# Sums of a softmax over 32 columns instead of 64, at another place, in a two-layer attention kernel

## The reference

```python
xn = _group_norm(xf, gamma, beta)
qkv = jnp.einsum('oc,bcl->bol', w_qkv, xn) + b_qkv[None, :, None]
q, k, v = jnp.split(qkv, 3, axis=1)           # each to (b*8, 64, 1024)
weight = jnp.einsum('bct,bcs->bts', q * scale, k * scale)
weight = jax.nn.softmax(weight.astype(jnp.float32), axis=-1)
a = jnp.einsum('bts,bcs->bct', weight, v)
hid = jnp.einsum('oc,bcl->bol', w_proj, a.reshape(b, c, L)) + b_proj[None, :, None]
return (xf + hid).reshape(b, c, h, w)
```

## Time and profile before

| | us |
|---|---|
| median of 3 runs | 2539.09 |
| the profiled execution | 2540.45 |
| its span, first to last instruction | 2537.3 |
| PE busy | 2466.6 (97%) |
| DVE busy | 1728.9 (68%) |
| POOL busy | 1234.4 (49%) |
| ACT busy | 1161.3 (46%) |

### The profile page before, as it was taken

One profiled execution on the slowest core, in us unless ns is written; L12 is line 12 of the kernel. 1 busy time (PEld: TensorE's weight loads), 2 busy tenths in 40 slices (PEclk: granted clock), 3 DMA queues, 4 the chain that ended last, 5 costly groups with the idle time before them and its releaser, 6 DMA issues.

```text
span 2537.3 us, 37438 instructions
## 1 busy us (share of the span) xinstructions
PE 2466.6 (97%) x12980; PEld 1618.3 (64%) x12980; DVE 1728.9 (68%) x2226; ACT 1161.3 (46%) x1499; POOL 1234.4 (49%) x621
## 2 busy tenths in 40 slices
PE   7999999999799999999999999999999999999987
PEld 6887888878555575557556655755565565557544
DVE  6455554546568866885787588578857866885776
ACT  3332232322355535654555455355555645553553
POOL 3330000000066746774766567377656756771762
PEclk9999999999899999999999999999999999999999
DMA  5431111013221141114022220502230241202001
GB/s 191 141 108 50 50 66 66 33 50 116 88 79 50 76 183 50 83 49 176 26 100 104 104 108 17 207 26 83 92 133 26 100 169 56 84 30 104 17 17 67
DMA packets 64185, 214.15 MB, mean 84 GB/s; under 512 B 9152, under 2 KB 9152, under 8 KB 63168
## 3 DMA queue, kind: packets, MB, share of 16 engines
q1 hardware_dynamic: 49504, 159.41, 17.1%
q0 software_dynamic: 14560, 52.96, 5.7%
HBM read 141.05 MB, written 71.30 MB: 84 GB/s over the span
## 4 chain that ended last, share of the span: by engine, by line
PE 82%; issue 8%; POOL 4%; DVE 3%; ACT 2%; POOLq 0%; ACTq 0%; DVEq 0%
PE psum L1258 16%; PE psum L1445 14%; PE psum L1507 14%; PE psum L1489 11%; PE psum L1277 7%; PE psum L1456 5%; POOL a_all L566 4%; PE psum L1301 4%; PE psum L1329 3%; PE psum L1521 3%; PE psum L1375 1%; ACT a_all L783 1%; PE psum L1269 1%; PE psum L1543 1%; PE psum L1389 1%
## 5 line engine op out<-in xcount | busy, mean ns | idle before, releaser
L566 POOL TENSOR_TENSOR a_all<-a_all 128x1024 f32<-128x1024 f32 x441 | 1059.9, 2403 | 500.2 <-ACT a_all L783 462.4
L783 ACT ACTIVATE a_all<-psum 128x1024 f32<-128x1024 f32 x512 | 496.6, 1022 | 65.8 <-PE psum L1489 51.9
L1507 PE MATMUL psum<-a_all 128*64 128x512 f32 x2048 | 495.7, 605 | 0.0
L1069 DVE TENSOR_REDUCE small<-psum 128x2 f32<-128x1024 f32 x326 | 399.7, 1226 | 125.6 <-PE psum L1456 123.1
L1258 PE MATMUL psum<-r_all 128*128 128x512 f32 x1920 | 455.8, 396 | 6.9 <-DVE r_all L1148 5.8
L1489 PE MATMUL psum<-r_all 64*128 64x512 f32 x3200 | 423.6, 395 | 4.5 <-ACT a_all L783 2.3
L1258 PEld LDWEIGHTS psum<-r_all 128*128 128x128 f32 x1920 | 360.4, 190 | 103.1 <-DVE r_all L922 10.2
L1445 PE MATMUL psum<-r_all 128*128 128x512 f32 x1536 | 372.2, 399 | 5.5 <-DVE r_all L1166 5.5
L1489 PEld LDWEIGHTS psum<-r_all 64*128 64x128 f32 x3200 | 295.5, 185 | 92.1 <-ACT a_all L783 35.6
L1445 PEld LDWEIGHTS psum<-r_all 128*128 128x128 f32 x1536 | 284.4, 189 | 104.2 <-issue 42.9
L1507 PEld LDWEIGHTS psum<-a_all 128*64 128x64 f32 x2048 | 124.0, 136 | 235.2 <-issue 170.7
(11 more groups left out here) (144 smaller groups left out, 2495.5 us busy)
## 6 DMA issues: line engine op xcount, KB each, us to landing
r_all<-w_dram SPq DMA_DIRECT2D x48, 1024.0 KB, 4.9
xn_dram<-a_all POOLq DMA_DIRECT2D x56, 512.0 KB, 5.4
r_all<-xn_dram SPq DMA_DIRECT2D x7, 4096.0 KB, 15.4
a_all<-y_dram SPq DMA_DIRECT2D x9, 2048.0 KB, 8.6
a_all<-x SPq DMA_DIRECT2D x16, 1024.0 KB, 6.4
y_dram<-a_all SPq DMA_DIRECT2D x16, 1024.0 KB, 4.2
out<-a_all SPq DMA_DIRECT2D x32, 512.0 KB, 4.0
w_dram<-a_all POOLq DMA_DIRECT2D x16, 512.0 KB, 3.0
```

Of the source, the lines that this page charges most:

```text
L566: pool.tensor_tensor(p_sum[:, :, cols], probs[:, 0, :, cols] if i == 1 else p_sum[:, :, cols], probs[:, i % SLOTS, :, cols], ALU.add).then ...
L783: act.activation(probs[:, i % SLOTS, :, cols], psum[half][:, :, :], ACT.Exp, scale=SCALE).then_inc(probs_ready, 1)
L1069: dve.reduce_max(max2[:, :, tile, half], psum[3][:, :, :], AX_X).then_inc(work_free, 2)
L1507: last = pe.matmul(psum[2][h * D:(h + 1) * D, half], v_t[:, i, head], probs[:, i % SLOTS, h, half * HALF:(half + 1) * HALF], start=(i == 0 ...
```

## The change

- `sums` makes four products of 32 columns instead of 64. Product k (head k // 2, half k % 2 of the queries) writes partitions 32k to 32k + 31 of one bank. The last pair of all keeps the old form.
- Its place: in pairs 1 to 3 behind the first score tile (bank psum[2][:,0]); in the last pair of the last batch behind the third (psum[3][:,0]); for pair 3 behind the third value tile instead of the second, into psum[2][:,0].
- ACT copies 128x512 to a new tile sums4, behind the first score tile's exps. DVE inverts it in 4 pieces. SP then issues 8 DMAs per pair (`spread`), each of 32 partitions x 512 floats, from sums4 to the two 32-partition parts of recip that hold one head and half. `normalise` waits for them (recip_spread).
- The first two output tiles of a batch (but the last) are made in two parts: both take their banks first, then each gets the products over the first three blocks of hid, then each the last.
- The mask is [128, 8] float32, read with stride 0, instead of [128, 1024] bfloat16.
- Waits: the first score tile no longer waits for `sums_copied`; the second key tile of a pair does, for an older copy, and the first value product does for this one.

```diff
@@ sync: issued in the middle of pairs 1 to 3, and behind the residual's load
+            def spread(b, p):
+                pairs = b * PAIRS + p
+                sp.wait_ge(sums_inverted, (pairs + 1) * PIECES)
+                sp.wait_ge(o_normed, NORMED0 + pairs * NH)
+                for k in range(2 * NH):
+                    for r in range(2):
+                        at = k // NH * D + r * QUARTER
+                        sp.dma_start(recip[at:at + QUARTER, k % NH], sums4[k * QUARTER:(k + 1) * QUARTER]).then_inc(recip_spread, 16)
@@ scalar
-                act.wait_ge(o_normed, NORMED0 + pairs * NH)
+                act.wait_ge(recip_spread, ONE + pairs * SPREAD)
                 act.wait_ge(sums_full, ONE + pairs + 1)
-                act.activation(recip, psum[1][:, :, :], ACT.Copy).then_inc(sums_copied, 1)
+                act.activation(sums4, of, ACT.Copy).then_inc(sums_copied, 1)
...
-                        if p and i == 2:
-                            copy_sums(b, p - 1)
...
+                        if p and more and i == 0:
+                            copy_sums(b, p - 1, psum[2][:, 0])
+                        if p and not more and i == 2:
+                            copy_sums(b, p - 1, psum[3][:, 0])
@@ vector
-                            if p and (m == 1 or m and m % 2 == 0):
-                                invert_sums(b, p - 1, m // 2, 1)
+                            if p and m in (2, 4, 6, 8):
+                                invert_sums(b, p - 1, m // 2 - 1, 1)
...
-                        if 1 <= i <= 4:
-                            invert_sums(b, PAIRS - 1, 2 * (i - 1), 2)
+                        if i in (2, 3):
+                            invert_sums(b, PAIRS - 1, 2 * (i - 2), 2)
                         if i == 5:
                             for h in range(NH):
                                 normalise(b, PAIRS - 1, h)
@@ tensor
-                for half in range(NH):
-                    for h in range(2):
-                        last = pe.matmul(psum[1][h * D:(h + 1) * D, half], ones64, p_sum[:, h, half * HALF:(half + 1) * HALF],
-                                         start=True, stop=True)
+                for k in range(2 * NH):
+                    h, half = k // NH, k % NH
+                    to = psum[1][h * D:(h + 1) * D, half] if last else to_bank[k * QUARTER:(k + 1) * QUARTER]
+                    done = pe.matmul(to, ones64[:, 0:D if last else QUARTER], p_sum[:, h, half * HALF:(half + 1) * HALF],
+                                     start=True, stop=True)
...
-                    if p:
-                        sums(pairs - 1)
                     next_qk(3)
                     next_max()
                     for i in range(NT):
                         scores(pairs, par, i, more)
+                        if p and more and i == 0:
+                            pe.wait_ge(k_free[1], pairs + 2)
+                            sums(pairs - 1, psum[2][:, 0])
+                        if p and not more and i == 2:
+                            sums(pairs - 1, psum[3][:, 0])
...
+                if not last:
+                    pe.wait_ge(ws_loaded[0], (loads + 3) * 16)
+                    hid_made(PAIRS - 1, NH - 1)
+                    banks = [next_tile() for _ in range(NH)]
+                    for (o, half), to in zip(tiles, banks):
+                        proj_steps(to, o, half, range(CT - 1))
+                    for (o, half), to in zip(tiles, banks):
+                        hid_made(PAIRS, half)
+                        proj_steps(to, o, half, (CT - 1,)).then_inc(work_full, 1)
```

More of the change, by code:

```diff
@@ L23 @@
 F32R = mybir.dt.float32r
-BF16 = mybir.dt.bfloat16
 ALU = mybir.AluOpType
@@ L450, in batch1 @@
                     load_y(b + 2)
+                spread(b, 0)
                 sp.wait_ge(qk_hi_done, qk_used(b, 2))
@@ L467, in batch1 @@
                 sp.dma_start(res32, y_v[b]).then_inc(res_loaded, 16)
+                if not last:
+                    spread(b, PAIRS - 1)
                 for o in range(CT):
@@ L1128, in normalise @@
                     dve.wait_ge(o_ready, ONE + pairs + 1)
-                dve.wait_ge(sums_inverted, pairs * PIECES + (h + 1) * CT)
+                if last:
+                    dve.wait_ge(sums_inverted, pairs * PIECES + h + 1)
+                elif h == 0:
+                    dve.wait_ge(recip_spread, ONE + (pairs + 1) * SPREAD)
                 o32 = o32s[:, p % 2, cols]
@@ L1509, in weigh, with sums @@
                 last.then_inc(pv_done, 1)
-            def sums(pairs, last=False):
+            def sums(pairs, to_bank, last=False):
                 pe.wait_ge(probs_ready, ONE + (pairs + 1) * 2 * NT)
@@ L1617, in batch1, with proj_steps @@
                         v_tile(i)
-                        if i == 1:
-                            sums(b * PAIRS + PAIRS - 1)
-                for t, (o, half) in enumerate(proj_tiles(last)):
+                        if i == 2:
+                            pe.wait_ge(o_ready, ONE + (b + 1) * PAIRS)
+                            sums(b * PAIRS + PAIRS - 1, psum[2][:, 0])
+                def proj_steps(to, o, half, js):
                     cols = slice(half * HALF, (half + 1) * HALF)
                     slot, piece = o // 2, o % 2
-                    if o == 0:
-                        pe.wait_ge(hid_lo_done, HID0 + (b + 1) * PAIRS * NH - (NH - 1 - half))
-                    if half == 0 and piece == 0:
-                        n_load = (loads + 3 + slot) - (1 if last and slot else 0)
-                        pe.wait_ge(ws_loaded[slot], n_load * 16)
-                    product(next_tile(), [(w_s[:, slot, piece, w, j], hid[:, m, j, cols])
-                                          for j in range(CT) for w, m in THREE]).then_inc(work_full, 1)
+                    for j in js:
+                        for k, (w, m) in enumerate(THREE):
+                            done = pe.matmul(to, w_s[:, slot, piece, w, j], hid[:, m, j, cols], start=(j == 0 and k == 0),
+                                             stop=(j == CT - 1 and k == 2))
+                    return done
@@ new lines, in hid_made @@
+                def hid_made(pairs, half):
+                    pe.wait_ge(hid_lo_done, HID0 + (b * PAIRS + pairs) * NH - (NH - 1 - half))
+                tiles = proj_tiles(last)
+                if not last:
+                    pe.wait_ge(ws_loaded[0], (loads + 3) * 16)
[6 more added lines that the diff above has]
+                        proj_steps(to, o, half, (CT - 1,)).then_inc(work_full, 1)
@@ L1632, in _ @@
+                for o, half in tiles[0 if last else NH:]:
+                    if o == 0:
+                        hid_made(PAIRS, half)
+                    if half == 0 and o % 2 == 0:
+                        n_load = (loads + 3 + o // 2) - (1 if last and o // 2 else 0)
+                        pe.wait_ge(ws_loaded[o // 2], n_load * 16)
+                    proj_steps(next_tile(), o, half, range(CT)).then_inc(work_full, 1)
             with nc.Fori(0, B - 1, engines=[pe.engine], hint_back_edge=True) as b:
```

55 lines of the change are left out of this document (32 added, 23 removed).

## The result

The changed kernel takes 2560.36 us (median of 4 runs, 2556.35 to 2561.01) against 2539.66 for the kernel before (median of 4 runs here): ratio 1.008 (95% interval 1.0062 to 1.0097), slower by 20.7 us. 2511 was forecast, with a range of 2502 to 2529.

What follows compares the result with a forecast made beforehand. PE, busy 97% of the span, was taken as the bound. Gains of 8.3 + 6.4 + 7.7 + 4 + 2 = 28.4 us from 2540.45 gave 2512.0, or 2510.7 against the median; predicted 2511, range 2502 to 2529.

Steps and rivals of the forecast that it cites:

- The sums themselves: Sums' matmuls: all four products run together, two rounds, 0.91 us instead of 1.87; 1.1 with shape changes.
- rival A: Sums: the four products don't run four at a time and stay at 1.87 us plus shape changes; 2537 us, chance 0.12.
- Where they stand: Sums behind the first score tile fill idle PE: gain 0.55 us in pairs 2 and 3, 0.8 in pair 1.
- Behind the third value tile: Value tiles after pair 3: no wait for POOL, 2.35 us gained, less new output-tile waits; 1.1 per batch, 7.7 in all.
- the two parts: First two output tiles: PE waits at least 1.0 us for the eighth value copy, some 0.25 for the third tile's bank.
- The spread: SP's eight DMAs per pair: free within pairs; behind the value tiles issued by 1145.6, landed at 1148, just fitting.
- rival B: Behind the value tiles the spread lands late, holding DVE's normalise and the last value copies: 2567 us, slower, chance 0.08.
- The last pair: Last pair of the last batch: sums behind the third score tile, DVE's adds start sooner; gain 4 us, 2 to 6.
- The start: Kernel start: smaller mask shortens PE's 8.88 us wait for POOL's constants; gain 2.0 us, bounds 1.3 and 2.5.

Runs made afterwards that it cites:

- place_old: Changed kernel, but in pairs 1 to 3 the 32-column sums stand between the third and fourth projection tile, as before the change: 2548.28 us against 2560.36.
- direct: Changed kernel, but pair 3's sums, behind the third value tile, keep the old 64-column form without spread: 2526.14 us, ratio 0.9946.
- mask_alone: Kernel before the change with only the small mask added: 2537.48 us against 2540.27, ratio 0.999.
- pool_later: Changed kernel, but GpSimd's two 512 KB stores and its load behind the value tiles start only once pair 3's spread has landed: 2532.80 us, ratio 0.9968.

## Why the prediction was wrong

Step by step, as the prediction put them:

- *The sums themselves*: right. Eight matmuls in 0.99 to 1.0 us before the next group starts; rival A (two at a time, 1.87) is out. Four matmuls start within 0.02 us, the next four 0.45 later. The prediction weighed two places of the Trainium skill ("TensorE: Matmul & The Clock Gate"): the faulty fourth column group ("Step-by-step: what each phase is for") shows nothing here, and the packing gain of four by four ("Measured speedup vs the span model") agrees with four at a time.
- *Where they stand*: the mechanism was right, the size not. The first max tile moved to 12.2 behind the pair's first projection matmul, as forecast (12.3). Behind it 0.38 instead of 0.55 was kept in pairs 2, and 0.45 instead of 0.8 in pairs 1 (batches 0 to 5; 1.1 in batches 6 and 7): the third max tile waits for DVE's reduction of the second and comes 5.17 behind the first, where the working has it at 4.97. The working compared DVE with the second max tile and did not follow it to the third. And it never priced the narrow sums at the old place: by its own terms that is 1.96 - 1.1 = 0.86, more than the 0.55 it came to, and 'place_old' shows 0.9.
- *Behind the third value tile*: right up to the output tiles: no wait for POOL, the eighth value tile ends about 2 sooner, 0.8 waiting for its copy (1.0 forecast). But the two parts were booked with 1.25 in all and cost 1.6, since the bank of the third tile was put at 0.25 and the output tiles grew by 0.6.
- *The spread*: this is the step that failed. It was named, with its place and its price (a microsecond of PE for each one beyond 1148.4), as rival B at 0.08, and the price held: DVE's normalise started at 1152.2, 3.8 beyond, and PE idled 5.1, which is 4.1 over the 1.0. What was mis-sized is the time on the queue. Eight issues were put at 0.38 each, from a row of a 2 MB load; an issue of 32 rows inside SBUF takes 0.62 (4.95 for eight, in every pair, undisturbed) and 0.9 beside GpSimd's and the residual's transfers. 3.0 forecast, 7.2 measured; the landing 2.5 forecast, 3.0 measured. At the undisturbed price, 4.95 and a landing of 2.0, the spread would by estimate have been there at 1148.9, half a microsecond late; the rest of the lateness goes with the other transfers. I had looked only at what was ahead on SP's own queue and not at GpSimd's stores, which are issued 0.9 and 0.3 us before the first of the eight. In the forecast's own terms this cost 34.0 - 7 x 1.0 = 27, and the clock behind the idle, which no term held, 12 more: the output tiles of batches 0 to 5 take 23.9 to 25.0 each, against 22.4 in 'direct'. The decision point of rival B, a landing at 1153, was too late because it left the clock out.
- *The last pair*: right in kind: 5.2 against 4, though 'mask_alone', whose code is the old one there, also shows 1.2 less. *The start*: 2.8 against 2.0: PE started at 6.38, when the first half of x had landed, instead of 8.88. The size lies within what this stretch varies by.
- *Batch 6*: no step held it: +6.8 from a stop of DVE that the kernel before has as well, 1.5 long, at a place where PE doesn't wait for it.

Without the late spread the sum comes near: 'direct' less what DVE's stop took there (53.07 against 45.69) is 2519, 8 above the forecast of 2511. A spread in time would keep the sums of pair 3 at 1.0 instead of 1.9, by estimate 6 less in seven batches.

## What to carry to other kernels

A detour by DMA between two engines costs its issues before it costs its latency: count them one by one, at the price of a row of the same shape, and add every transfer of every queue that is in flight there, also those that your path doesn't wait for. Narrower sums and a better place are two edits; measure each alone, since here the first gave 0.9 us a pair and the second took back 0.5 in most of them. And where PE idles for some microseconds, add what the lower clock takes behind it: here 1.5 to 2.6 us behind an idle of over 5, and in 'pool_later' 1.5 in two of six batches behind idles of about 2.

## What the runs showed of the hardware that was not expected

- Four float32 products of 32 columns, on four quarters of the output partitions, run side by side: 1.0 us for eight passes, against 1.87 with 64 columns two by two.
- One DMA of 64 KB inside SBUF costs its queue 0.62 us (a load of 1 or 2 MB 0.38), and 0.9 to 1.2 with other transfers or a second issuing queue beside it; it lands a median of 2.0 us after its issue.
- DVE stops once for 1.5 to 5.5 us in batch 6, whose code stands outside the loop, the kernel before included; in the one kernel with 16 instructions ahead of it the stop no longer shows.
